# The first sweep of a four-layer graph kernel with split operands, and remainders taken by two engines

## The chip, the cores and the metric

The kernel runs on one core of one Trainium2 chip. The metric is the device time of one launch in microseconds (us): 1341.96 us, the median of three runs (1341.93 to 1343.07) of the kernel before. A profile of one further execution, of 1341.3 us, is what the traces below come from; its span, from the first instruction to the last, is 1339.5 us, so 1.8 us lie around it.

## What is computed

The input is x (4096 x 128) and a dense float32 matrix adj (4096 x 4096, 64 MB). Four graph layers follow each other, each closed by a residual and a layer norm:

```python
x = _layernorm(x + _L0_gnn_ref(x, adj, ...))   # (adj @ x + beta*x) / (rowsum(adj) + beta) @ kernel + bias
x = _layernorm(x + _L1_gnn_ref(x, adj, ...))   # h = relu(adj @ (h @ W) + b), three times, widths 20, 20, 128
x = _layernorm(x + _L2_gnn_ref(x, adj, ...))   # D^-1/2 adj D^-1/2 @ (x @ W + b), D = rowsum(adj)
x = _layernorm(x + _L3_gnn_ref(x, adj, ...))   # adj @ x + gamma * softmax((x@W_l)(x@W_r)^T) @ x @ W_h @ W_g
```

So adj is read six times: once for layer 0, three times for layer 1, once each for layers 2 and 3. The row sums of adj are needed after the first of these readings.

## The kernel before

Each reading of adj is a sweep, s = 0 to 5. A sweep has eight rows c of 512 output nodes, and a row has eight blocks d of 512 input nodes, in two halves h: a tile is 128 x 1024 float32 (512 KB), a row has 16 tiles, a sweep 128. Tiles stream through a ring `raw` of 8 slots; SyncE (SP) issues the loads, waiting for a slot with `wait_ring`. In every row two blocks (four tiles, `KEPT`) are held in SBUF through the sweeps 0 to 3 and not loaded again; only those of row 1 (`LATE`) are streamed in sweep 0 and loaded into their place afterwards by `load_late`.

Sweeps 1 to 3 are narrow (20 columns of TensorE) and share tiles: `joined` says which tiles of a sweep also serve the product of the next sweep, and such a joint tile is used twice and not read again. In sweep 0, row c has c joint blocks (all d below c), whose second product goes to the bank `ahead`, which ScalarE copies to `sums` in `store_ahead`. `FILL` names rows whose held tiles TensorE works off between the sweeps 0 and 1, where it waits for the last row's layer norm.

Sweep 0 (`first_sweep`, L1298) multiplies in plain float32: two 128x512 matmuls per tile, each recorded as two. VectorE does nothing for this product; it adds up the tiles for the row sums (`row_sum`, L867, 15 additions per row, then `fold`, L872), which TensorE sums over partitions with a column of ones (L1207). The wide sweeps 4 and 5 instead split each operand in two parts, hi and lo, of a format that TensorE multiplies faster: ScalarE copies the tile to `t_hi` (L743), VectorE subtracts (`t_lo`, L1029), and TensorE does three products per 512 columns (L1449, L1450, L1454). ScalarE may be at most HL = 4 tiles ahead of TensorE there. In the attention of layer 3, ScalarE and GpSimd split the exponentials (L799, L613) while VectorE works on scores in PSUM (L1081, L1103).

Each engine has its own in-order queue, written out by hand. The work that ends a row (its epilogue) is threaded through the next row at fixed tile numbers: TensorE's `epilogue_1` after tile 1, `epilogue_3` after 9, `epilogue_4` after 11; VectorE's residual, statistics and scales between its additions; GpSimd's three small operations per row: `bx` (L578), `xb` (L555) and the copy of the new x (L583).

## Time and profile before

| | us |
|---|---|
| median of 3 runs | 1341.96 |
| profiled execution | 1341.3 |
| its span | 1339.5 |
| TensorE (PE) busy | 1285.0 (96%) |
| VectorE (DVE) busy | 930.6 (69%) |
| ScalarE (ACT) busy | 715.7 (53%) |
| GpSimd (POOL) busy | 267.5 (20%) |
| end of the first sweep | about 291 |
| first wide matmul (sweep 4) | about 531 |

The stretches: sweep 0 up to 291 us, the narrow sweeps up to 531 us, the wide sweeps up to about 905 us, then attention. TensorE is nearly always busy, so its own durations and short waits set the end; VectorE has little to spare in the wide sweeps and much in sweep 0. TensorE's matmuls overlap in the records, so the time one costs is read from start to start, not from its duration.

### The profile page before, as it was taken

How to read it: one execution, taken by the hardware profiler on the slowest of the kernel's cores; microseconds unless marked ns; L12 is line 12 of the kernel's file. 1: busy time of each engine (PE TensorE's matmuls, PEld its weight loads, DVE VectorE, ACT ScalarE, POOL GpSimd, SP SyncE). 2: the span in 40 equal slices, each digit the busy share in tenths (PEclk: the TensorE clock that was granted, in tenths of full speed). 3: DMA queues.
4: the chain of work that ended last, by engine and by line, in shares of the span. 5: the costliest groups of instructions: out<-in, count | busy, mean ns of one | idle time of the engine just before them, and what ended most of it. 6: DMA issues, size and time to landing. Idle time of an engine off the chain costs nothing.

```text
span 1339.5 us, 17278 instructions
## 1 busy us (share of the span) xinstructions
PE 1285.0 (96%) x5911; PEld 792.2 (59%) x5911; DVE 930.6 (69%) x1207; ACT 715.7 (53%) x880; POOL 267.5 (20%) x175
## 2 busy tenths in 40 slices
PE   8999999999999899999999999998899999999987
PEld 3544444433232233778787788886677767767764
DVE  6666665551010365999999989896888788788885
...
GB/s 367 314 316 251 251 219 204 173 188 181 382 333 400 309 352 407 307 353 374 351 371 359 376 356 361 382 291 0 1 0 1 1 1 1 1 18 14 1 1 32
DMA packets 81087, 288.01 MB, mean 215 GB/s; under 512 B 9466, under 2 KB 11130, under 8 KB 81018
## 3 DMA queue, kind: packets, MB, share of 16 engines
...
q8 instruction: 41, 0.67, 0.2%
...
HBM read 284.98 MB, written 2.10 MB: 214 GB/s over the span
## 4 chain that ended last, share of the span: by engine, by line
PE 79%; DVE 8%; ACT 4%; issue 4%; DMA 3%; POOL 1%; POOLq 0%; ACTq 0%; DVEq 0%; SPq 0%
PE acc L1298 17%; PE acc L1536 7%; PE acc L1454 7%; PE acc L1388 7%; PE acc L1449 6%; PE acc L1450 6%; DMA raw<-in_adj_s 3%; DVE t_lo L1029 2%; PE rs L1306 2%; PE acc L1526 2%; PE acc L1527 2%; PE acc L1530 2%; PE e L1491 2%; PE e L1493 2%; PE rs L1491 2%
## 5 line engine op out<-in xcount | busy, mean ns | idle before, releaser
L1029 DVE TENSOR_TENSOR t_lo<-raw,t_hi 128x1024 fp32r<-128x1024 f32 x256 | 311.1, 1259 | 26.7 <-ACT t_hi L743 21.8
L743 ACT ACTIVATE t_hi<-raw 128x1024 fp32r<-128x1024 f32 x256 | 261.5, 1054 | 40.5 <-PE acc L1454 39.9
L1449 PE MATMUL acc<-t_hi,st_hi 128*128 128x512 f32 x512 | 201.9, 394 | 0.9 <-ACT t_hi L743 0.9
L1450 PE MATMUL acc<-t_hi,st_lo 128*128 128x512 f32 x512 | 199.5, 390 | 0.0
L613 POOL TENSOR_TENSOR ring_lo<-ring,p_hi 128x1024 fp32r<-128x1024 f32 x64 | 155.4, 2429 | 220.0 <-ACT p_hi L799 219.9
L1298 PE MATMUL acc<-raw,x 128*128 128x512 f32 x400 | 179.3, 597 | 0.0
L1454 PE MATMUL acc<-t_lo,st_hi 128*128 128x512 f32 x512 | 159.5, 393 | 5.8 <-DVE t_lo L1029 5.0
L1103 DVE TENSOR_TENSOR ring<-ring,e 128x1024 f32<-128x1024 f32 x128 | 154.0, 1212 | 0.1
L793 ACT ACTIVATE ring<-ring 128x1024 f32<-128x1024 f32 x128 | 134.2, 1054 | 25.0 <-DVE ring L1103 24.9
L1298 PEld LDWEIGHTS acc<-raw,x 128*128 128x128 f32 x400 | 73.7, 190 | 92.0 <-issue 92.0
L1536 PE MATMUL acc<-ring,x 128*128 128x512 f32 x256 | 120.2, 592 | 0.0
L583 POOL COPY x<-xn 128x512 f32<-128x512 f32 (+1 forms) x24 | 20.4, 850 | 485.5 <-ACT xn L683 485.5
L867 DVE TENSOR_TENSOR rsum<-rsum,raw 128x1024 f32<-128x1024 f32 x86 | 109.1, 1269 | 11.0 <-DMA raw<-in_adj_s 5.5
L1454 PEld LDWEIGHTS acc<-t_lo,st_hi 128*128 128x128 f32 x512 | 95.0, 188 | 30.7 <-DVE t_lo L1029 11.4
L1449 PEld LDWEIGHTS acc<-t_hi,st_hi 128*128 128x128 f32 x512 | 96.1, 188 | 21.8 <-DVE st_lo L877 1.3
L1450 PEld LDWEIGHTS acc<-t_hi,st_lo 128*128 128x128 f32 x512 | 96.2, 188 | 19.7 <-issue 0.2
L1081 DVE TENSOR_TENSOR peak<-e,peak 128x1024 f32<-128x1024 f32 x54 | 66.1, 1223 | 41.0 <-ACT ring L805 40.8
L892 DVE TENSOR_TENSOR at<-acc,sums 128x512 f32<-128x512 f32 x20 | 13.8, 689 | 113.7 <-PE acc L1388 87.8
L1081 DVE TENSOR_TENSOR peak<-rs,peak 128x1024 f32<-128x1024 f32 x61 | 74.5, 1222 | 24.9 <-ACT ring L805 24.6
L1388 PE MATMUL acc<-raw,h_a 128*20 128x512 f32 x384 | 81.3, 596 | 2.4 <-DMA raw<-in_adj_s 1.3
L805 ACT ACTIVATE ring<-rs 128x1024 f32<-128x1024 f32 x62 | 63.3, 1021 | 36.5 <-PE rs L1493 36.4
L1491 PE MATMUL e<-q_hi,k_hi 128*128 128x512 f32 x122 | 70.0, 573 | 3.5 <-DVE peak L1081 1.9
...
## 6 DMA issues: line engine op xcount, KB each, us to landing
...
```

The source lines that it names most:

```text
L613: nc.gpsimd.tensor_tensor(ring_lo[:, n % RING, :], slot(n), p_hi[:, m % 2, :].bitcast(F32), ALU.subtract).then_inc(pl_done, 1)
L743: nc.scalar.activation(t_hi[:, g % HL, :], raw[:, k, :], ACT.Copy).then_inc(hi_done, 1)
L793: nc.scalar.activation(slot(n), slot(n), ACT.Exp).then_inc(exped, 1)
L1029: nc.vector.tensor_tensor(t_lo[:, k, :], raw[:, slot_no(s, c, g), :], t_hi[:, k, :].bitcast(F32), ALU.subtract).then_inc(lo_done, 1)
L1081: nc.vector.tensor_tensor(peak[:, :], score_bank(t)[:, :], peak[:, :], ALU.max).then_inc(s_maxed, 1)
L1103: nc.vector.tensor_tensor(part, part, row, ALU.subtract).then_inc(subbed, 1)
L1298: m = mm(a[:, :], block_of(x0, i.d * CB + i.h * GB + j), t[:, j * CW:(j + 1) * CW], start=(n == 0 and j == 0), stop=False)
L1388: m = mm(a[k:k + H, :], h[:, b * H:(b + 1) * H], t[:, j * CW:(j + 1) * CW], start=(i.d == items[0].d), stop=(i.d == items[-1].d))
L1449: mm(a[:, :], block_of(st_h, b), hi[:, m], start=(g == 0 and j == 0), stop=False)
L1450: mm(a[:, :], block_of(st_l, b), hi[:, m], start=False, stop=False)
L1454: i = mm(a[:, :], block_of(st_h, b), lo[:, m], start=False, stop=(g == NG - 1 and j == GB - 1))
L1536: r = mm(o, block_of(x, b), slot(n)[:, u * CW:(u + 1) * CW], start=(b == 0), stop=(b == NB - 1))
```

## The change

Sweep 0 is split as sweeps 4 and 5 are. ScalarE writes `x_hi` (in four parts) and a `t0_hi` for each of the 128 tiles, a remainder `t_lo` is subtracted for each, and TensorE does three products in place of the plain one. The remainders are shared by a table `POOL_LO`: GpSimd takes 9, 10, 9, 8, 8, 6, 4, 4 of the 16 in rows 0 to 7 (58 in all), VectorE the other 7, 6, 7, 8, 8, 10, 12, 12 (70). VectorE also subtracts the four parts of `x_lo`.

The row sums of joint tiles no longer come from VectorE: the stationary operand of the joint product gets a 21st column of ones, and `epilogue_1` adds the sums that this gives by four more small products with `row_picker`. VectorE's additions fall from 15 in every row to 15, 13, 11, 9, 7, 5, 3, 1.

The split needs room, so the held tiles of rows 0 to 3 are streamed in sweep 0 and loaded again after it (16 late tiles, 4 before), and `FILL` names rows 4 and 5 in place of 0 and 2. ScalarE's 16 loads of constants, issued at the head before, now stand between the tiles 4 and 5 of its first row.

VectorE's queue for the first sweep's row 1, up to its fifth addition. Before (L867 adds a tile to the row sums, L916 and L939 are the residual):

```order
L863 TENSOR_TENSOR rsum<-raw 128x1024
L867 TENSOR_TENSOR rsum<-rsum,raw 128x1024
L900 TENSOR_TENSOR deg<-e,beta 128x4
L901 TENSOR_SCALAR dg<-sq 128x4
L903 RECIPROCAL inv<-deg 128x4
L905 RECIPROCAL dinv<-dg 128x4
L916 TENSOR_TENSOR xs<-e,inv 128x512
L867 TENSOR_TENSOR rsum<-rsum,raw 128x1024
L939 TENSOR_TENSOR xs<-xs,xb 128x512
L867 TENSOR_TENSOR rsum<-rsum,raw 128x1024
```

And of the change (L1005 is a remainder, L987 the addition):

```order
L1005 TENSOR_TENSOR t_lo<-raw,t_hi 128x1024
L983 TENSOR_TENSOR rsum<-raw 128x1024
L987 TENSOR_TENSOR rsum<-rsum,raw 128x1024 x2
L1005 TENSOR_TENSOR t_lo<-raw,t_hi 128x1024
L987 TENSOR_TENSOR rsum<-rsum,raw 128x1024
L1053 TENSOR_TENSOR deg<-e,beta 128x4
L1054 TENSOR_SCALAR dg<-sq 128x4
L1056 RECIPROCAL inv<-deg 128x4
L1058 RECIPROCAL dinv<-dg 128x4
L1069 TENSOR_TENSOR xs<-e,inv 128x512
L987 TENSOR_TENSOR rsum<-rsum,raw 128x1024
```

The remainders stand between the additions, each ahead of the addition of its tile; both kinds read two tensors in SBUF.

GpSimd's queue from its first operation on. Before (rows 0 and 1 of the sweep):

```order
L578 TENSOR_TENSOR bx<-x,beta 128x512
L555 TENSOR_TENSOR xb<-x,bias 128x512
L578 TENSOR_TENSOR bx<-x,beta 128x512
L583 COPY x<-xn 128x512
L555 TENSOR_TENSOR xb<-x,bias 128x512
```

And of the change (the same two rows):

```order
L635 TENSOR_TENSOR t_lo<-raw,t_hi 128x1024 x3
L649 TENSOR_TENSOR bx<-x,beta 128x512
L635 TENSOR_TENSOR t_lo<-raw,t_hi 128x1024 x7
L621 TENSOR_TENSOR xb<-x,bias 128x512
L635 TENSOR_TENSOR t_lo<-raw,t_hi 128x1024 x2
L649 TENSOR_TENSOR bx<-x,beta 128x512
L635 TENSOR_TENSOR t_lo<-raw,t_hi 128x1024 x5
L654 COPY x<-xn 128x512
L635 TENSOR_TENSOR t_lo<-raw,t_hi 128x1024 x3
```

The small operations stay; 19 remainders are put around them in the two rows (the last of the three shown at the end is row 2's).

ScalarE's queue at the start of the change, where the constants' loads now stand:

```order
L794 ACT_TABLE_LOAD
L794 ACTIVATE x_hi<-x 128x1024
L805 ACTIVATE t_hi<-raw 128x1024 x4
L794 ACTIVATE x_hi<-x 128x1024
L805 ACTIVATE t_hi<-raw 128x1024
L809 DMA comb<-in_comb 128x128
L809 DMA k<-in_L_gnn_kernel 128x128
```

They were ahead of everything; five tiles of the split now stand before them.

The diff, cut to its core:

```diff
-LATE = 1
-FILL = {0: (0, 1), 2: (2, 3)}
+LATE = (0, 1, 2, 3)
+FILL = {4: (4, 5), 5: (5,)}
...
-    return d in KEPT[c] and not (s == 0 and c == LATE)
+    return d in KEPT[c] and not (s == 0 and c in LATE)
...
-        mine = {1: [6, 7, 5], 2: [1, 0, 3, 2]}[s]
+        mine = {1: [6, 7], 2: [1, 0, 3, 2]}[s]
...
+PLAIN = [[n for n, i in enumerate(ITEMS[0, c]) if not i.fused] for c in range(NC)]
+POOL_LO = ((1, 2, 4, 6, 7, 9, 11, 12, 14), (0, 2, 3, 5, 7, 8, 10, 12, 13, 15), (0, 2, 4, 6, 8, 10, 11, 13, 15),
+           (0, 2, 4, 6, 8, 10, 12, 14), (0, 2, 4, 6, 8, 10, 12, 14), (0, 3, 6, 9, 12, 15), (1, 5, 9, 13), (1, 5, 9, 13))
...
+        row_folded = sums[:, 0, :]
+        row_picker = comb[:, H:HA]
...
                     if i.seq == t:
-                        sp.wait_ge(sum_done, r * NSUM + max(n, 1))
-            sp.wait_ge(pe_tile, t + 1)
+                        wait_lo(sp, c, n)
+                        if i.fused:
+                            sp.wait_ge(pe_tile, JOINT_AT[c, n])
+                        else:
+                            sp.wait_ge(sum_done, sums_through(c, n))
+                        return
...
-                for d in KEPT[LATE]:
-                    for h in range(2):
-                        sp.dma_start(kept_tile(LATE, d, h), tile(LATE, 2 * d + h)).then_inc(late_in, 16)
+                for c in reversed(LATE):
+                    for d in KEPT[c]:
+                        for h in range(2):
+                            sp.dma_start(kept_tile(c, d, h), tile(c, 2 * d + h)).then_inc(late_in[c], 16)
...
+                u = c * NG + n
+                pool.wait_ge(hi_done, u + 1)
+                nc.gpsimd.tensor_tensor(t_lo[:, u % HL, :], tile_of(0, c, ITEMS[0, c][n]),
+                                        t0_hi[:, u % HL, :].bitcast(F32), ALU.subtract).then_inc(lo_pool_done, 1)
+
+            def first_row(c):
+                for n in range(NG):
+                    if n == 1 and c > 0:
+                        if c == 1:
+                            for part in range(1, XP):
+                                pool.wait_ge(x_in[part], 16)
+                        keep_old_x(0, c - 1)
+                    if n == 5:
+                        if c > 0:
+                            pool.wait_ge(pe_acc, c)
+                            alone(pool)
+                        nc.gpsimd.tensor_tensor(blocks(bx[:, :]), blocks(cols(x, c)), spread(cols(beta, c, CB)),
+                                                ALU.mult).then_inc(S["bx"], 1)
+                    if n == 13 and c > 0:
+                        pool.wait_ge(S["norm"], done("norm", 0, c - 1))
+                        alone(pool)
+                        nc.gpsimd.tensor_copy(cols(x, c - 1), xn[:, :]).then_inc(S["xw"], 1)
...
+                act.wait_ge(x_in[part], 16)
+                nc.scalar.activation(cols(x_hi, part, NB * D // XP), cols(x, part, NB * D // XP),
+                                     ACT.Copy).then_inc(x_hi_done, 1)
+
+            def first_row(c):
+                for n, i in enumerate(ITEMS[0, c]):
+                    u = c * NG + n
+                    if c == 0 and n % (NG // XP) == 0:
+                        operand_hi(n * XP // NG)
+                    wait_tile(act, 0, c, i)
+                    if u >= HL:
+                        act.wait_ge(pe_tile, SPLIT_AT[divmod(u - HL, NG)])
+                    nc.scalar.activation(t0_hi[:, u % HL, :], tile_of(0, c, i), ACT.Copy).then_inc(hi_done, 1)
+                    if c == 0:
+                        if n == 4:
+                            for dst, src in consts:
+                                nc.scalar.dma_start(dst[:, :], src).then_inc(const_in, 16)
+                        continue
+                    if n == 2:
+                        evacuate(0, c - 1, 1 - c % 2)
+                        store_ahead(0, c - 1)
+                    if n == 4:
+                        second(0, c - 1)
+                    if n == 8:
+                        deviation(0, c - 1)
+                    if n == 10:
+                        normalise(0, c - 1)
+                    if n == 12:
+                        transposed(0, c - 1)
+                if c > 0:
+                    next_h(0, c - 1)
+
...
                 nc.scalar.dma_start(dst[:, :], src).then_inc(first_in, 16)
-            act.wait_ge(x_in[1], 16)
-            for dst, src in consts:
-                nc.scalar.dma_start(dst[:, :], src).then_inc(const_in, 16)
-            for part in range(XP):
-                act.wait_ge(x_in[part], 16)
-                nc.scalar.activation(cols(x, part, NB * D // XP), cols(x0, part, NB * D // XP),
-                                     ACT.Copy).then_inc(x_all, 1)
...
-
-            def row_sum(c, n):
-
-                mine, other = ITEMS[0, c][0], ITEMS[0, c][n + 1]
+            nc.vector.memset(h_a[:, :], 1.0).then_inc(memset_done, 1)
+
+            def row_sum(c, k):
+
...
+                if c > 0:
+                    dve.wait_ge(S["mm1"], done("mm1", 0, c) - 1)
+                nc.vector.tensor_tensor(row_folded, rsum[:, 0:CW], rsum[:, CW:2 * CW],
                                         ALU.add).then_inc(S["rr"], 1)
+
+            def operand_lo(part):
+                dve.wait_ge(x_hi_done, part + 1)
+                nc.vector.tensor_tensor(cols(x_lo, part, NB * D // XP), cols(x, part, NB * D // XP),
+                                        cols(x_hi, part, NB * D // XP).bitcast(F32), ALU.subtract).then_inc(x_lo_done, 1)
+
+            def remainder(c, n):
+                u = c * NG + n
+                dve.wait_ge(hi_done, u + 1)
+                nc.vector.tensor_tensor(t_lo[:, u % HL, :], tile_of(0, c, ITEMS[0, c][n]),
+                                        t0_hi[:, u % HL, :].bitcast(F32), ALU.subtract).then_inc(lo_done, 1)
+
+            def first_row(c):
+                for n in range(NG):
+                    if c == 0 and n % (NG // XP) == 0:
+                        operand_lo(n * XP // NG)
+                    if n not in POOL_LO[c]:
+                        remainder(c, n)
+                    if n in PLAIN[c][1:]:
...
+                        if n == 4:
+                            residual_1(0, c - 1)
...
                         mm(e0[:, b * D:(b + 1) * D], block_of(at, b), k0[:, :], start=True, stop=True)
+                    if stored(0, c):
+                        pe.wait_ge(sums_done, stored(0, c))
                     for b in range(CB):
-                        i = mm(e1[:, b:b + 1], block_of(rsum, b), ones_f[:, 0:1], start=True, stop=True)
+                        i = mm(e1[:, b:b + 1], block_of(row_folded, b), ones_f[:, 0:1], start=True,
+                               stop=not stored(0, c))
+                        if stored(0, c):
+                            i = mm(e1[:, b:b + 1], block_of(sums[:, c, :], b), row_picker, start=False, stop=True)
...
-                        pe.wait_ge(x_in[i.d * XP // NC], 16)
-                    wait_tile(pe, 0, c, i)
-                    t = tile_of(0, c, i)
+                        pe.wait_ge(x_lo_done, i.d * XP // NC + 1)
+                    hi, lo = t0_hi[:, n % HL, :], t_lo[:, n % HL, :]
+                    pe.wait_ge(hi_done, c * NG + n + 1)
                     for j in range(GB):
-                        m = mm(a[:, :], block_of(x0, i.d * CB + i.h * GB + j), t[:, j * CW:(j + 1) * CW],
-                               start=(n == 0 and j == 0), stop=False)
+                        b, m = i.d * CB + i.h * GB + j, slice(j * CW, (j + 1) * CW)
+                        mm(a[:, :], block_of(x_hi, b), hi[:, m], start=(n == 0 and j == 0), stop=False)
+                        mm(a[:, :], block_of(x_lo, b), hi[:, m], start=False, stop=False)
+                    wait_lo(pe, c, n)
+                    for j in range(GB):
+                        b, m = i.d * CB + i.h * GB + j, slice(j * CW, (j + 1) * CW)
+                        k = mm(a[:, :], block_of(x_hi, b), lo[:, m], start=False, stop=False)
...
     for j in range(4):
-        arrays["comb"][32 * j:32 * j + H] = np.eye(H, P, dtype=np.float32)
+        arrays["comb"][32 * j:32 * j + HA] = np.eye(HA, P, dtype=np.float32)
```

## Rows read from the trace of the kernel before

**Rows 1.** Windows, one row of sweep 0: us, then busy of each engine (instructions), clock, DMA

```profile
74.00:108.00 34.00, 34.00 (x120) 16.23 (x116) 23.01 (x33) 3.95 (x10) 4.17 (x3) 1.00 0.67 257
```

**Rows 2.** Timeline of TensorE in sweep 0: start, length, engine, line, instructions

```profile
6.56 9.73 PE L1298 MATMUL acc<-kept_x,x 128*128 128x512 f32 x16 [6.56 <-DMA kept_x<-in_adj_s]
...
42.76 13.98 PE L1298 MATMUL acc<-raw,x 128*128 128x512 f32 x32
56.57 0.60 PE L1245 MATMUL e<-ident,xn 128*128 128x128 f32 x4
...
75.79 0.95 PE L1207 MATMUL e<-ones_f,rsum 128*128 128x1 f32 x8
...
211.76 1.16 PE L1325 MATMUL acc<-ident,bx 128*128 128x128 f32 x8
...
290.00 1.16 PE L1325 MATMUL acc<-ident,bx 128*128 128x128 f32 x8
```

**Rows 3.** Timeline of TensorE in sweep 4: the first product of two tiles that follow

```profile
573.88 0.39 PE L1449 MATMUL acc<-t_hi,st_hi 128*128 128x512 f32 x1
...
575.24 0.39 PE L1449 MATMUL acc<-t_hi,st_hi 128*128 128x512 f32 x1
```

**Rows 4.** Timeline of GpSimd in sweep 0

```profile
36.90 1.27 POOL L555 TENSOR_TENSOR xb<-x,bias 128x512 f32<-128x512 f32 x1 [8.89 <-DMA gamma<-in_L_gnn_gamma]
38.12 1.04 POOL L578 TENSOR_TENSOR bx<-x,beta 128x512 f32<-128x512 f32 x1
...
55.74 1.08 POOL L583 COPY x<-xn 128x512 f32<-128x512 f32 x1 [16.58 <-ACT xn L683]
56.99 2.04 POOL L555 TENSOR_TENSOR xb<-x,bias 128x512 f32<-128x512 f32 x1 [0.17 <-POOL x L583]
```

**Rows 5.** Instances of VectorE's addition: ns min/median/max, starts; all, then 56.5 to 58.0

```profile
L867 DVE TENSOR_TENSOR rsum<-rsum,raw x86: 1215/1225/2103, 12.8 to 274.9; 128x1024 f32<-128x1024 f32 x86
...
L867 DVE TENSOR_TENSOR rsum<-rsum,raw x2: 1443/1773/2103, 56.5 to 58.0; 128x1024 f32<-128x1024 f32 x2
```

**Rows 6.** Timeline of GpSimd and VectorE at two places of the attention

```profile
931.53 2.40 POOL L598 TENSOR_TENSOR x<-x,ones_f 128x1024 f32<-128x1024 f32 x1
...
932.30 1.92 DVE L1069 TENSOR_TENSOR v_lo<-x,v_hi 128x256 fp32r<-128x256 f32 x1
...
1310.94 2.41 POOL L613 TENSOR_TENSOR ring_lo<-ring,p_hi 128x1024 fp32r<-128x1024 f32 x1
...
1311.91 1.99 DVE L1119 TENSOR_TENSOR xf<-o_s,xf 128x512 f32<-128x512 f32 x1
```

**Rows 7.** Instances of two lines of the attention: ns min/median/max, starts

```profile
L1119 DVE TENSOR_TENSOR xf<-o_s,xf x8: 691/693/1990, 1011.5 to 1331.8; 128x512 f32<-128x512 f32 x8
...
L613 POOL TENSOR_TENSOR ring_lo<-ring,p_hi x64: 2376/2400/2741, 951.3 to 1323.3; 128x1024 fp32r<-128x1024 f32 x64
```

**Rows 8.** The page's groups: line, engine, count, then busy us and mean ns

```profile
L743 ACT ACTIVATE t_hi<-raw 128x1024 fp32r<-128x1024 f32 x256 | 261.5, 1054 | 40.5 <-PE acc L1454 39.9
...
L1103 DVE TENSOR_TENSOR ring<-ring,e 128x1024 f32<-128x1024 f32 x128 | 154.0, 1212 | 0.1
```

**Rows 9.** Timeline of ScalarE at the start: its loads of constants and what follows

```profile
11.56 0.33 ACTq L772 DMA_DIRECT2D comb<-in_comb  x1
...
20.14 1.28 ACT L775 ACT_TABLE_LOAD   x1 [20.14 <-issue]
```

**Rows 10.** Timeline of SyncE: the late loads and the first load after them

```profile
291.19 1.75 SPq L494 DMA_DIRECT2D kept_late<-in_adj_s  x4
312.23 87.60 SPq L513 DMA_DIRECT2D raw<-in_adj_s  x58
```

**Rows 11.** Windows of three stretches, columns as in rows 1

```profile
302.00:303.00 1.00, 0.67 (x4) 0.56 (x3) 0.00 (x0) 0.24 (x1) 0.00 (x0) 0.50 0.00 0
...
430.00:440.00 10.00, 10.00 (x82) 3.25 (x78) 0.69 (x1) 1.39 (x3) 0.00 (x0) 1.00 1.03 410
...
458.00:460.00 2.00, 0.00 (x0) 0.00 (x0) 1.50 (x11) 0.24 (x2) 0.00 (x0) 1.00 1.00 338
```

191 lines of the change are left out of this document (111 added, 80 removed).

## The prediction, made before the changed kernel was run

> **What bounds the kernel now.** I read the page's engine totals first, then the windows of sweep 0, then TensorE's timeline there, and last the places where GpSimd and VectorE work at once. The windows show TensorE busy all the time in sweep 0 (34.00 of 34 us) and VectorE 23.01 us of it [rows 1]. TensorE's starts give the price of its work: 32 recorded plain matmuls, eight tiles, take from 42.76 to 56.57, so 1.73 us per tile. Rows 6 and 7 of the sweep together take from 211.76 to 290.00, 78.2 us, and the sweep ends at 291.2 [rows 2]. In sweep 4 a tile of the split form takes from 573.88 to 575.24, 1.36 us [rows 3]. So TensorE bounds sweep 0 before, and the split takes 0.37 us off each of its 128 tiles: 47 us, if TensorE goes on being the bound. The question is whether it does.
>
> **What the remainders cost.** Take a row before: 23.0 us of VectorE with 15 additions of 1.225 us [rows 1, 5], so 4.6 us are for the rest. After, a row has additions plus VectorE's remainders, 1.22 us each (both are subtractions or additions of the same shape). These are 22, 19, 18, 17, 15, 15, 15, 13 in rows 0 to 7, and row 0 has four x_lo besides. Alone that gives 27.8, 26.6, 25.3, 22.9 (three times) and 20.5 us for rows 1 to 7. TensorE's row falls by 16 x 0.37 = 5.9 us and gains, from row 2 on, the four products with row_picker, which are like the four of 75.79: 0.95, less overlap 0.85 [rows 2]. Rows 6 and 7 come to 78.2 - 11.7 + 1.7 = 68.2; a row has one joint block more than the one before it, 1.2 us by the same timeline's step, so rows 1 to 5 are about 27, 29, 30, 31, 32.5. If GpSimd's share ran freely beside VectorE's, VectorE would thus be just under or at TensorE.
>
> It does not run freely in this trace. GpSimd's xb takes 1.27 us at 36.90, where VectorE is idle, and 2.04 us at 56.99, where VectorE is adding [rows 4]. At the same moment one of VectorE's additions takes 2.10 instead of 1.225, and the one before it, which meets GpSimd's copy of 55.74, takes 1.44 [rows 5]. Each waits for the other: xb ends at 59.03, the addition started at 58.0 cannot run until about 58.9. In the attention it is the same with a long GpSimd operation: the one of 1310.94 ends at 1313.35, and VectorE's 1311.91, which is 0.69 us alone, takes 1.99 and ends just after; that of 931.53 ends at 933.93 and VectorE's of 932.30 takes until 934.22 [rows 6, 7]. The attention's other VectorE work reads one tensor in PSUM and one in SBUF, and with 64 GpSimd remainders around, its 128 instances have a mean of 1.21 us: no delay [rows 7, 8]. In sweep 0 of the change VectorE's additions and remainders all have both inputs in SBUF, and GpSimd's remainders too. The Trainium skill says why (page "SBUF — State Buffer", section "Who interferes with whom"): a VectorE instruction with two SBUF inputs uses the read port it shares with GpSimd, and whoever starts first has it for the whole instruction. By that rule the two engines' times add and sharing the remainders gains nothing; by the view that engines run side by side, sweep 0 would come out as in the first rival. The rows above agree with the rule.
>
> So a GpSimd remainder costs VectorE its own length nearly. From xb: 0.88 us lost for an operation of 1.27 us, and a remainder of 2.40 us [rows 7] is 1.13 longer: 2.0. The upper bound is the whole length, 2.4; the lower is the part that falls where VectorE waits anyway, nothing. I take 2.1, near what the rows measure.
>
> **The sum of sweep 0.** Row 0: the first tile is there at 6.56 [rows 2], one ScalarE copy of 1.05 us [rows 8] follows, so 7.6. Then 26 operations of VectorE (31.7), the fold 0.7, bx 0.9 (1.04 alone, rows 4), 9 GpSimd remainders of 2.1 (18.9): 52.2. ScalarE's 16 loads of constants take from 11.56 to 20.14, 8.6 us [rows 9]; between tiles 4 and 5 they stop t_hi for that long. ScalarE waited for the second part of x until 11.56 before; from there two copies (2.1), the loads (8.6) and the next copy (1.05) put tile 5's t_hi at 23.3. The eight VectorE operations (9.8) and three GpSimd remainders (6.3) that stand before it take from 7.6 to 23.7, so they cover the loads and I count nothing; if the engines ran side by side, 6 us of it would show. Row 0 ends at 59.8.
> Rows 1 to 5, VectorE's own time + 0.9 for bx + GpSimd's 10, 9, 8, 8, 6 remainders: 49.7, 46.4, 43.0, 40.6, 36.4, together 216.1. About 1.5 us per row of VectorE's small operations (they read PSUM or one tensor) can lie beside GpSimd's: 208.6.
> Rows 6 and 7: VectorE and GpSimd need 22.9 + 0.9 + 8.4 = 32.2 and 29.8, TensorE 68.2 for both and is the bound; with ScalarE only four tiles ahead and each remainder waiting its turn I add 1 us per row: 70.2.
> End of sweep 0: 59.8 + 208.6 + 70.2 = 338.6, against 291.2 before: 47.4 us later.
>
> **The other parts.** The loads of sweep 0 keep up: it moves the same 64 MB in more time. After it, SyncE issues 16 late loads where it issued 4, ahead of the next ring loads. Before, it issued nothing from 293 to 312.23 [rows 10]; at 410 GB/s a tile is 1.28 us [rows 11], so the 12 more take 15.4 us and fit into that gap of 19. Later the narrow sweeps are near the DMA limit, so a remnant could count: 0 to 3 us. FILL has 12 block products where it had 16, so TensorE has 0.9 us less to do while it waits for the last layer norm, and its rows 5 and 4 of sweep 1 get shorter and hide less of their own epilogues: 0 to 2 us. I take 1.5 for all of it. A second memset, the wider h_a and the 21st column cost nothing on the path: TensorE's first product waits for a tile anyway, and even in proportion to the columns the 28 joint blocks of 1.2 us would be 1.7 us longer in all. The wide sweeps and the attention are unchanged.
> Sum: 1341.3 + 47.4 + 1.5 = 1390 for an execution like the profiled one, whose time is 0.7 us below the median; so 1391.
>
> **The rivals.**
> First, the engines do not block each other here, and the kernel is faster. Row 0 is then VectorE's 32.4 us from 7.6 on, with 6 us idle behind the constants: 46.5. In rows 1 to 3 VectorE (28, 27, 25) has little to do until ScalarE has copied out the last row (two copies half as wide as a t_hi, and the t_hi itself: 0.6 + 0.6 + 1.05), which costs about 4 us a row: some 32 each. Rows 4 to 7 are TensorE's, about 31 + 32.5 + 68.2. End at 275 to 276, 15.5 us earlier, and 1341.3 - 15.5 + 1.5 = 1327. For it: the remainder of 2.40 us is short enough that 10 in a row fit beside. Against it: rows 4 to 6, three separate places. It decides if a remainder costs VectorE less than 0.9 us.
> Second, half the blocking: 1.0 us per remainder, since VectorE waits in part of each row anyway. Rows 0 to 5 have 50 of them, so rows 0 to 3 come to 49.9 (from the start), 37.2, 35.0 and 32.7, rows 4 and 5 to TensorE's 31 and 32.5, and with 70.2 for the last two the end is 288.5: 1341.3 - 2.7 + 1.5 = 1340, no change. Nothing in the rows shows such a half; the row starts, where VectorE waits for the copies, speak for a part of it.
> Third, TensorE's clock. It fell to 0.50 of full speed (1.2 GHz) at 302, after 4 us in which TensorE was mostly idle, and held 1.00 in the stretch around 458 to 460 with an idle of 3 us [rows 11]. In rows 1 to 3 of the change TensorE has 27 to 30 us of work in 43 to 50. If it fell in each gap, a tile would be 2.7 us and a row about 53 to 60: rows 1 to 4 would be 4 to 20 us longer each, 1440 in all. Against it: the gaps are short, one per tile or two.
>
> **How the numbers follow.** Forecast 0.80, first rival 0.08, second 0.07, third 0.05. The forecast's own range: 50 remainders at 2.0 to 2.4 are -5 to +15, the small operations 0 to 2.8 us a row are +-7, the constants and the narrow sweeps +8: 1378 to 1412. With part of the second rival (a remainder at 1.5 us: 30 us less) the range is 1362 to 1412. A difference of 0.2%, 2.7 us, is about what can be told from no change here: slower 0.87 (the forecast, the third, a part of the second), same 0.05 (the second), faster 0.08 (the first).
>
> **What the profile after would show.** VectorE's additions and remainders in sweep 0 with a mean well above 1.22, near 2; GpSimd's remainders near 3 us, not 2.40; sweep 0 ending near 339; TensorE waiting for `t_lo` by GpSimd and VectorE through rows 1 to 5, and hardly in rows 6 and 7; its tile at 1.36 us where it does not wait. If VectorE's mean stays at 1.23 while GpSimd is at work, the forecast is wrong and the first rival holds; if VectorE is slowed but has idle time in rows 1 to 5, the second; a clock well under 1.00 in sweep 0 speaks for the third.

## The result, and the profile after

The changed kernel takes 1424.5 us (median of four runs, 1422.7 to 1426.8), the kernel before 1342.0 (four runs): a ratio of 1.062 with a 95% interval of 1.060 to 1.064. That is 82 us slower, where 49 were forecast; the time lies above the range. The profiled execution has a span of 1420.9 us, 81.4 more than before.

Windows of the changed kernel, one per row of sweep 0, each from the first product of one row's bx to that of the next; columns as in [rows 1].

```profile
0.00:58.47 58.47, 32.45 (x97) 23.81 (x97) 53.37 (x30) 25.19 (x24) 34.39 (x16) 0.82 0.72 256
58.47:114.31 55.84, 38.48 (x142) 28.64 (x140) 52.50 (x40) 20.46 (x26) 38.23 (x15) 0.76 0.43 142
114.31:165.48 51.17, 34.96 (x161) 24.95 (x157) 43.57 (x36) 19.67 (x26) 30.87 (x13) 0.87 0.49 164
165.48:209.77 44.29, 35.08 (x169) 24.85 (x165) 36.94 (x35) 19.56 (x26) 29.06 (x12) 0.92 0.65 238
209.77:251.51 41.74, 35.30 (x176) 24.33 (x173) 35.94 (x35) 19.66 (x26) 26.28 (x11) 0.92 0.53 202
251.51:294.08 42.57, 36.19 (x184) 24.12 (x180) 33.97 (x34) 19.92 (x26) 21.13 (x9) 0.88 0.53 197
294.08:331.62 37.54, 34.67 (x192) 23.09 (x188) 29.97 (x33) 19.94 (x26) 15.53 (x7) 1.00 0.59 225
331.62:366.88 35.26, 35.26 (x200) 23.32 (x196) 23.97 (x30) 16.88 (x23) 12.08 (x6) 1.00 0.61 209
```

In [rows 1] TensorE was busy in every microsecond of a row and VectorE had a third of it free. Now only row 7 is TensorE's. In row 1 VectorE is busy 52.50 of 55.84 us with 40 recorded instructions; before it did 33 in 23.0 us. The last bx products start at 366.88, where they started at 290.00 in [rows 2]: 76.9 us of the 81.4 are lost in sweep 0.

The page's groups that answer to [rows 5, 8]: line, engine, shapes and count, then busy us and mean ns, then idle time before them.

```profile
L635 POOL TENSOR_TENSOR t_lo<-raw,t_hi 128x1024 fp32r<-128x1024 f32 x53 | 155.2, 2938 | 120.9 <-ACT t_hi L805 120.9
...
L1450 PE MATMUL acc<-t_lo,x_hi 128*128 128x512 f32 x256 | 93.6, 451 | 61.0 <-DVE t_lo L1005 53.6
...
L1005 DVE TENSOR_TENSOR t_lo<-raw,t_hi 128x1024 fp32r<-128x1024 f32 x59 | 96.1, 1646 | 28.7 <-ACT t_hi L805 28.5
...
L987 DVE TENSOR_TENSOR rsum<-rsum,raw 128x1024 f32<-128x1024 f32 x46 | 95.8, 2082 | 2.2
```

VectorE's addition of 1.225 us now has a mean of 2.08, its remainder one of 1.65; GpSimd's remainder takes 2.94 where the same shape took 2.40 in the attention [rows 7]. The timeline of GpSimd and VectorE at the start of row 1 shows how they take turns:

```profile
58.93 6.13 POOL L635 TENSOR_TENSOR t_lo<-raw,t_hi 128x1024 fp32r<-128x1024 f32 x2
60.09 2.78 DVE L994 TENSOR_TENSOR sums<-rsum 128x512 f32<-128x512 f32 x1
62.79 3.35 DVE L1005 TENSOR_TENSOR t_lo<-raw,t_hi 128x1024 fp32r<-128x1024 f32 x1
65.03 2.02 POOL L649 TENSOR_TENSOR bx<-x,beta 128x512 f32<-128x512 f32 x1
66.07 2.06 DVE L983 TENSOR_TENSOR rsum<-raw 128x1024 f32<-128x1024 f32 x1
```

The fold of 60.09, 0.69 us alone, takes 2.78; VectorE's remainder of 62.79 takes 3.35 and ends 1.1 us (about one remainder's length) after GpSimd's second one at 65.06; GpSimd's bx, 1.04 us alone [rows 4], then takes 2.02. Small operations can be held too. Two lines of VectorE with four elements per partition (ns min/median/max), the first reading two tensors, the second one:

```profile
L1119 DVE SCALAR_TENSOR_TENSOR nmr<-mv,rstd x24: 161/162/2154, 88.6 to 813.2; 128x4 f32<-128x4 f32 x24
```

```profile
L1054 DVE TENSOR_SCALAR dg<-sq x8: 155/160/2279, 73.0 to 372.0; 128x4 f32<-128x4 f32 x8
```

Their longest instances both end with a remainder of GpSimd. Beside each stands a small operation that ran at its own length while the same remainder was under way: L1053, which reads one tensor in PSUM and one in SBUF, and L1117, which reads one in SBUF:

```profile
71.86 3.43 POOL L635 TENSOR_TENSOR t_lo<-raw,t_hi 128x1024 fp32r<-128x1024 f32 x1 [4.82 <-ACT t_hi L805]
72.97 0.15 DVE L1053 TENSOR_TENSOR deg<-e,beta 128x4 f32<-128x4 f32 x1
73.04 2.28 DVE L1054 TENSOR_SCALAR dg<-sq 128x4 f32<-128x4 f32 x1
...
88.20 2.49 POOL L635 TENSOR_TENSOR t_lo<-raw,t_hi 128x1024 fp32r<-128x1024 f32 x1 [5.93 <-ACT t_hi L805]
88.37 0.17 DVE L1117 RECIPROCAL rstd<-std 128x4 f32<-128x4 f32 x1
88.57 2.14 DVE L1119 SCALAR_TENSOR_TENSOR nmr<-mv,rstd 128x4 f32<-128x4 f32 x1
```

VectorE is not always busy or held. In rows 1 to 5 it is idle 32.7 us, and 27.4 us of that are two waits for ScalarE (total, times, longest):

```profile
DVE t_lo L1005 <- ACT t_hi L805: 19.1, 5, 6.8
DVE deg L1053 <- ACT sq L752: 8.3, 3, 3.5
```

Four of the five waits for t_hi, 17.8 us, stand where rows 2 to 5 begin: ScalarE writes three t_hi of the new row, then waits for TensorE's last product of the old row, copies it out, and only then writes the next t_hi. Row 1 has no such wait. Laid over each other, the timelines of VectorE and GpSimd leave about 17 us in rows 1 to 5 in which neither works; in the rest of VectorE's idle time GpSimd works alone.

Behind sweep 0 little changed. SyncE's 16 late loads and its next ring load, which answer to [rows 10]:

```profile
368.07 1.75 SPq L562 DMA_DIRECT2D kept_t<-in_adj_s  x4
...
374.10 2.84 SPq L562 DMA_DIRECT2D kept_x<-in_adj_s  x4
390.04 10.09 SPq L579 DMA_DIRECT2D raw<-in_adj_s  x7
```

They end well before the next load is due, as forecast. The wide sweeps start at 608.4, 241.5 us after the last bx products; before it was 530.8 and 240.8. The remaining 3.8 us of the difference lie behind that point, where the two kernels have the same code: 812.5 us against 808.7. TensorE's granted clock is lower there in a few places of this execution: 0.92 and 0.74 in the 10 us from 1258.4 and from 1268.4, 1.00 at the same places before. At a third place TensorE has the same 16.16 us of work within 20, at a clock of 0.91 in this execution and 1.00 in one of the first five-row kernel below (h5):

```profile
1360.90:1380.90 20.00, 16.16 (x56) 10.50 (x55) 16.11 (x17) 17.52 (x19) 8.87 (x4) 0.91 0.00 0
```

```profile
1268.40:1288.40 20.00, 16.16 (x62) 10.47 (x61) 16.49 (x18) 17.80 (x19) 8.62 (x4) 1.00 0.00 1
```

That the clock makes the 3.8 us is likely, and not shown by an experiment.

### The profile page after: what moved, and what is told of

Same layout as the page of the kernel before. It is cut to its first block, busy times and chain, and to the rows that moved or that the text cites. A ratio compares the mean times of both kernels' runs of the same rounds, so it can differ in the third digit from the quotient of the medians.

```text
span 1420.9 us, 18453 instructions
## 1 busy us (share of the span) xinstructions
PE 1286.1 (91%) x6223; PEld 866.2 (61%) x6223; DVE 1059.0 (75%) x1226; ACT 843.3 (59%) x1008; POOL 443.7 (31%) x233
## 4 chain that ended last, share of the span: by engine, by line
PE 54%; DVE 25%; issue 9%; ACT 7%; DMA 4%; POOL 1%; SPq 0%; DVEq 0%; POOLq 0%; ACTq 0%
DVE rsum L987 8%; PE acc L1535 7%; PE acc L1601 6%; PE acc L1596 6%; PE acc L1597 6%; PE acc L1683 4%; DMA raw<-in_adj_s 3%; DVE peak L1222 3%; DVE t_lo L1005 2%; ACT ring L924 2%; DVE t_lo L1170 2%; DVE ring L1244 2%; PE rs L1540 2%; PE acc L1450 2%; ACT ring L912 2%
## 5 line engine op out<-in xcount | busy, mean ns | idle before, releaser
L1170 DVE TENSOR_TENSOR t_lo<-raw,t_hi 128x1024 fp32r<-128x1024 f32 x256 | 311.1, 1260 | 26.7 <-ACT t_hi L869 21.8
L869 ACT ACTIVATE t_hi<-raw 128x1024 fp32r<-128x1024 f32 x256 | 261.5, 1054 | 40.6 <-PE acc L1601 39.9
L635 POOL TENSOR_TENSOR t_lo<-raw,t_hi 128x1024 fp32r<-128x1024 f32 x53 | 155.2, 2938 | 120.9 <-ACT t_hi L805 120.9
L805 ACT ACTIVATE t_hi<-raw 128x1024 fp32r<-128x1024 f32 x112 | 116.2, 1056 | 98.3 <-PE acc L1450 90.5
L1450 PE MATMUL acc<-t_lo,x_hi 128*128 128x512 f32 x256 | 93.6, 451 | 61.0 <-DVE t_lo L1005 53.6
L1445 PE MATMUL acc<-t_hi,x_hi 128*128 128x512 f32 x256 | 115.4, 451 | 23.5 <-DVE x_lo L999 16.0
L672 POOL COPY x<-xn 128x512 f32<-128x512 f32 (+1 forms) x17 | 12.8, 752 | 351.3 <-ACT xn L772 351.3
L1005 DVE TENSOR_TENSOR t_lo<-raw,t_hi 128x1024 fp32r<-128x1024 f32 x59 | 96.1, 1646 | 28.7 <-ACT t_hi L805 28.5
L1446 PE MATMUL acc<-t_hi,x_lo 128*128 128x512 f32 x256 | 110.5, 432 | 0.0
L1450 PEld LDWEIGHTS acc<-t_lo,x_hi 128*128 128x128 f32 x256 | 52.1, 214 | 85.0 <-DVE t_lo L1005 65.4
L987 DVE TENSOR_TENSOR rsum<-rsum,raw 128x1024 f32<-128x1024 f32 x46 | 95.8, 2082 | 2.2
```

The lines of the kernel that those rows point to most:

```text
L635: nc.gpsimd.tensor_tensor(t_lo[:, u % HL, :], tile_of(0, c, ITEMS[0, c][n]), t0_hi[:, u % HL, :].bitcast(F32), ALU.subtract).then_inc(lo_p ...
L869: nc.scalar.activation(t_hi[:, g % HL, :], raw[:, k, :], ACT.Copy).then_inc(hi_done, 1)
L987: nc.vector.tensor_tensor(rsum[:, :], rsum[:, :], tile_of(0, c, other), ALU.add).then_inc(sum_done, 1)
L1170: nc.vector.tensor_tensor(t_lo[:, k, :], raw[:, slot_no(s, c, g), :], t_hi[:, k, :].bitcast(F32), ALU.subtract).then_inc(lo_done, 1)
L1450: k = mm(a[:, :], block_of(x_hi, b), lo[:, m], start=False, stop=False)
```

## The experiments

All start from the changed kernel unless it is said otherwise. The ledger they fill is this, in us per row (worked out from windows like those above; "1 to 5" is their sum):

| kernel | row 0 | rows 1 to 5 | row 6 | row 7 | last bx |
|---|---|---|---|---|---|
| before | 36.7 | 175.0 | 38.5 | 39.7 | 290.0 |
| changed | 58.5 | 235.6 | 37.5 | 35.3 | 366.9 |
| e1, no GpSimd remainder | 50.0 | 189.5 | 34.1 | 35.3 | 308.9 |
| e2, GpSimd writes only | 43.3 | 166.3 | 34.1 | 35.3 | 279.0 |
| e6, GpSimd reads one | 50.2 | 187.3 | 34.1 | 35.3 | 306.9 |
| e7, 25 instead of 41 in rows 1 to 5 | 57.4 | 211.1 | 34.7 | 35.3 | 338.5 |
| e9, three places | 57.8 | 236.7 | 36.2 | 35.3 | 365.9 |
| h6, five fp32 rows | 36.6 | 172.0 | 34.1 | 35.3 | 278.0 |

### All remainders on VectorE (e1)

```
-POOL_LO = ((1, 2, 4, 6, 7, 9, 11, 12, 14), (0, 2, 3, 5, ...
+POOL_LO = ((),) * 8
```

> All 128 remainders of sweep 0 on VectorE, none on GpSimd (GpSimd keeps bx, the copy of old x and the new x). Theory A (a GpSimd remainder stops VectorE for its own length, so it costs VectorE about as much as doing it itself, and in the four-tile window the two cannot lie beside each other): sweep 0 gets shorter although VectorE has 58 more operations of 1.2 us; VectorE's own work is then 51 us in row 0, 40, 37.5, 35, 33, 32.5 in rows 1 to 5 and TensorE's 34 to 35 sets rows 6 and 7, a sum of about 298, with waits at the row heads 300 to 312; whole kernel 1355 to 1368. Rival B (GpSimd's remainders are real help and the loss comes from the waits between engines alone): VectorE's busy time of 303 us in the changed kernel grows by 58 x 1.2 = 70 us less what it was blocked, sweep 0 ends at or behind 368 and the kernel is at 1424 or slower. Rival C (TensorE's clock sets it): VectorE's share falls but the granted clock stays at 0.76 to 0.92 in rows 0 to 5, and sweep 0 ends near 350.

Measured: 1359.9 us, ratio 1.014 (1.011 to 1.018). 58 more instructions on VectorE, 65 us less time. Windows of rows 1 to 3:

```profile
49.97:92.52 42.55, 31.88 (x142) 22.22 (x140) 42.27 (x51) 20.63 (x26) 4.97 (x3) 0.96 0.60 197
92.52:130.94 38.42, 31.28 (x160) 22.32 (x157) 36.22 (x46) 19.68 (x26) 3.99 (x3) 1.00 0.63 219
130.94:169.45 38.51, 32.53 (x169) 22.38 (x165) 34.00 (x44) 19.68 (x26) 3.99 (x3) 1.00 0.74 273
```

Row 1 has 51 recorded VectorE instructions in 42.27 us, where 40 took 52.50. Theory A holds in sign and size, B and C fall. The price follows: rows 1 to 5 are 46.1 us longer in the changed kernel, for 41 remainders on GpSimd; 1.12 us each, and with the 1.22 us that VectorE is spared, a GpSimd remainder costs 2.34 us of elapsed time. Its own length is 2.40. This is a mean: worked out row by row the price is 2.55, 2.64, 1.94, 1.92 and 2.66, since the waits of the rows differ as well and TensorE is busy 33.29 of the 33.93 us of row 5 here. How close it comes to 2.40 is in part chance.

VectorE waits here too, although GpSimd has no remainder. In rows 1 to 5 it is busy 173.5 of 189.5 us, and most of the 16.0 us between are the same two waits:

```profile
DVE deg L1052 <- ACT sq L751: 7.4, 4, 2.4
DVE t_lo L1004 <- ACT t_hi L804: 7.2, 4, 1.8
```

### GpSimd writes but does not read (e2)

```
-  nc.gpsimd.tensor_tensor(t_lo[...], tile, t0_hi[...], ALU.subtract)
+  if c < 6: nc.gpsimd.memset(v[:, 0:TW], 0.0); nc.gpsimd.memset(v[:, TW:2 * TW], 0.0)
+  nc.gpsimd.memset(t_lo[...], 0.0)
```

> Each of GpSimd's 58 remainders is replaced by fills with zero that read nothing from SBUF: of the remainder's place in all rows, and in rows 0 to 5 of two more 1024-wide pieces of a buffer that is not in use yet, so that GpSimd is busy about as long as before for each. Left out is the subtraction of those 58 tiles (their remainder counts as zero). Theory A (what stops VectorE is GpSimd's reading of two operands): VectorE's operations run at their own length again (t_lo and row sums near 1.2 us instead of means of 1.65 and 2.08), sweep 0 ends at 276 to 295. Rival B (a GpSimd operation of 2.4 us and more in a window of four tiles sets the pace, whoever blocks whom): VectorE's means fall but its idle time grows by as much, sweep 0 ends at 350 to 368.

Measured: 1327.4 us (one run). GpSimd is still busy for most of row 1 (31.01 of 35.85 us; 38.23 in the changed kernel, where its operations were held), and VectorE is hardly slowed. Windows of rows 1 and 4, and VectorE's remainder in the page:

```profile
43.27:79.12 35.85, 30.54 (x142) 22.66 (x140) 31.83 (x40) 20.73 (x26) 31.01 (x32) 0.95 0.69 236
...
144.74:176.58 31.84, 31.84 (x177) 23.05 (x173) 23.96 (x35) 20.34 (x27) 26.68 (x29) 1.00 0.73 281
```

```profile
L1011 DVE TENSOR_TENSOR t_lo<-raw,t_hi 128x1024 fp32r<-128x1024 f32 x59 | 72.1, 1227 | 40.9 <-ACT t_hi L811 40.6
```

The 40 instructions of row 1 that took 52.50 us take 31.83. So neither GpSimd's being busy nor the length of its work in the window of four tiles is the cause; its reading is. The whole time is that of the prediction's first rival (1327 us), which supposed no blocking. Its sweep 0 is not quite: it said 275 to 276 (its terms add up to 274), and here the sweep ends at 280, the last bx products of 278.99 included. So the equal whole is in part luck.

### GpSimd reads one operand (e6)

```
-  nc.gpsimd.tensor_tensor(t_lo[...], tile, t0_hi[...], ALU.subtract)
+  nc.gpsimd.tensor_copy(t_lo[...], t0_hi[...])
```

> GpSimd's 58 remainders are replaced by copies of t0_hi, which read one operand and write the same place; left out is the subtraction (the remainder of those 58 tiles is wrong). Theory A (a GpSimd operation holds VectorE's two-operand operations only where it itself reads two operands): VectorE's t_lo and row sums stay near 1.25 us and sweep 0 ends near 279, as with the fills. Rival B (any GpSimd read of SBUF holds them for its length): VectorE's means rise as in the changed kernel (1.65 and 2.08 us), less as far as the copy is shorter than 2.4 us, and sweep 0 ends at 310 to 368.

Measured: 1358.7 us (one run), the last bx at 306.9. The page's groups:

```profile
L635 POOL CAST t_lo<-t_hi 128x1024 fp32r<-128x1024 f32 x58 | 89.4, 1547 | 163.1 <-ACT t_hi L805 163.1
L1005 DVE TENSOR_TENSOR t_lo<-raw,t_hi 128x1024 fp32r<-128x1024 f32 x59 | 84.5, 1446 | 35.2 <-ACT t_hi L805 35.1
```

Theory A falls: the copy has a mean of 1.55 us (its shortest is 1.04), VectorE's remainder 1.45. A GpSimd operation that reads one operand in SBUF holds VectorE too, as B says, and in the mean for about its own length: rows 1 to 5 are 2.2 us shorter than in e1, so a copy costs 1.22 - 0.05 = 1.17 us against 1.04 alone. The end lies 3 us under B's 310; B had allowed for a shorter copy, but not for one this short.

### No GpSimd remainder at the rows' edges (e7)

```
-POOL_LO = (..., (0, 2, 3, 5, 7, 8, 10, 12, 13, 15), (0, 2, 4, 6, 8, 10, 11, 13, 15), ...
+POOL_LO = (..., (3, 5, 7, 8, 10, 12), (4, 6, 8, 10, 11), ...
```

> GpSimd takes no remainder among a row's first and last three tiles (rows 0 to 7: 8, 6, 5, 5, 5, 4, 2, 2 of 16 instead of 9, 10, 9, 8, 8, 6, 4, 4); VectorE does the others. In rows 1 to 5 these are 25 instead of 41. Between none (VectorE busy 173.5 us in these rows, idle 16.1) and 41 (202.9 and 32.7) a remainder on GpSimd costs 0.72 us of VectorE's busy time net. Theory A (the idle time of VectorE comes from GpSimd's remainders at the heads and ends of rows): busy about 191, idle 16 to 20, rows 1 to 5 take 207 to 211 us and sweep 0 ends at 335 to 345. Rival B (it comes with every remainder, wherever it stands): idle 26 or more, rows 1 to 5 take 217 or more, sweep 0 ends at 347 or later.

Measured: 1390.5 us (one run), the last bx at 338.5; rows 1 to 5 take 211.1, VectorE busy in 189.1 and idle in 22.0. The end fits A, the idle time lies between the two: the run does not tell them apart. Each of the 25 remainders costs (211.1 - 189.5) / 25 + 1.22 = 2.08 us, less than the 2.34 of those in the changed kernel.

### Three places instead of four (e9)

```
+HL0 = 3
-  t0_hi[:, u % HL, :] ... t_lo[:, u % HL, :]
+  t0_hi[:, u % HL0, :] ... t_lo[:, u % HL0, :]
```

> The changed kernel with three places for t0_hi and t_lo in sweep 0 instead of four, so that ScalarE may be three tiles ahead of TensorE. The work of every engine is the same. In rows 1 to 5 of the changed kernel VectorE was busy 202.9 us and idle 32.7, of that 19.1 in five waits for t_hi, one at each row's head, and 8.3 for ScalarE's square root there. Theory A (VectorE's idle time is a matter of the window: ScalarE cannot be far enough ahead to cover the last remainders, the copies out of the finished row and a GpSimd operation that stops VectorE): idle in rows 1 to 5 rises to 45 to 75 us, busy stays within 5 of 203, sweep 0 ends 15 to 50 us later, 382 to 417. Rival B (the idle time is the fixed chain at the head of a row, bx products, copy out, epilogue, whatever the window): idle stays at 30 to 38, sweep 0 ends at 365 to 375.

Measured: 1418.4 us (one run), the last bx at 365.9. VectorE's waits from 60 to 320 us (total, times, longest):

```profile
DVE t_lo L1006 <- ACT t_hi L806: 40.3, 17, 5.6
```

Neither theory fits as a whole: the time is B's (365 to 375), VectorE's idle and busy times are not, and A misses the time. VectorE is idle 44.0 us in rows 1 to 5 instead of 32.7, and busy 192.8 instead of 202.9; the sum is 236.7 instead of 235.6. With a smaller window VectorE spends as idle what it spent held by GpSimd: the timelines laid over each other have about 25 us of rows 1 to 5 in which GpSimd works and VectorE is idle, where the changed kernel has 14. The time in which neither works is about 17 us in both. So that part of VectorE's idle time is a cost, and the part beside a working GpSimd is not one of its own. The four places are not the bound.

### TensorE kept busy (e4)

```
+  if c < 6:
+      for j in range(GB):
+          mm(a[:, :], zeros_r[:, :], hi[:, j * CW:(j + 1) * CW], start=False, stop=False)
```

> In rows 0 to 5 two more products of 512 columns per tile, with a stationary of zeros, stand between the hi and the lo products, so that TensorE has fewer and shorter gaps; the sum is unchanged. At full clock they cost TensorE 0.43 us a tile, 1.79 instead of 1.36 us, 7 us a row, still below VectorE's time of the rows (42 to 58 us). Theory A (VectorE and GpSimd set the rows, the granted clock of 0.76 to 0.92 lies under that): the clock of rows 0 to 5 rises to 0.95 or more and sweep 0 ends within 5 us of 368, 363 to 375. Rival B (the slow products stand in the loop of the four-tile window, so the clock has a share of its own): sweep 0 ends 8 to 25 us earlier, 343 to 360, and the kernel is that much faster.

Measured: 1427.6 us, ratio 1.0645 (1.062 to 1.067). Windows of rows 4 and 5:

```profile
216.11:259.12 43.01, 39.92 (x209) 29.02 (x205) 34.63 (x34) 20.03 (x26) 25.24 (x10) 1.00 0.51 196
259.12:300.41 41.29, 40.81 (x216) 29.13 (x212) 29.93 (x34) 20.04 (x26) 21.81 (x9) 1.00 0.54 204
```

Rows 4 and 5 run at 1.00 instead of 0.92 and 0.88 and take 84.3 us together, as in the changed kernel. Rows 0 to 3 rose only to 0.86 to 0.93, short of the 0.95 expected, and row 3 took 49.5 us instead of 44.3, with more work for TensorE in it; the last bx products start at 373.2, 6.3 us later, within A's range. So the clock lies under VectorE and GpSimd in rows 4 and 5. For rows 0 and 1 the windows of the changed kernel say it, since VectorE is busy in all but 5.1 and 3.3 us of them. For rows 2 and 3 it is likely and not shown.

### Constants at the head of ScalarE's queue (e3)

```
+  for dst, src in consts: nc.scalar.dma_start(...)      # ahead of the first tile
```

> The 16 constant loads stand at the head of ScalarE's queue again instead of behind the fifth tile. In the changed kernel ScalarE wrote no t0_hi from 12.78 to 20.26 us while they were issued, and VectorE had no idle time then. Theory A (that stall lies under VectorE's own backlog): row 0 ends within 1.5 us of 58.5, with VectorE busy 53 us in it; the whole kernel within 3 us of 1424. Rival B (the stall holds the window of four tiles back): row 0 ends 4 to 7 us earlier, and the kernel gains as much.

Measured: 1426.5 us (one run). Row 0 ends at 65.0 instead of 58.5, which neither theory said: I had forgotten that the 16 issues now stand before the first x_hi. VectorE's start in both kernels, this one first:

```profile
12.42 1.23 DVE L998 TENSOR_TENSOR x_lo<-x,x_hi 128x1024 fp32r<-128x1024 f32 x1 [9.51 <-ACT x_hi L794]
```

```profile
6.14 1.22 DVE L999 TENSOR_TENSOR x_lo<-x,x_hi 128x1024 fp32r<-128x1024 f32 x1 [3.23 <-ACT x_hi L794]
```

From there to the end of row 0 it is 52.6 us here and 52.3 in the changed kernel. So the 7.5 us in which ScalarE issues them behind the fifth tile cost nothing that shows, as A says of the stall; its "within 1.5 us of 58.5" failed.

### The late loads alone (e5)

From the kernel before: LATE, FILL and what hangs on them.

```
-LATE = 1
-FILL = {0: (0, 1), 2: (2, 3)}
+LATE = (0, 1, 2, 3)
+FILL = {4: (4, 5), 5: (5,)}
```

> The kernel before with only the late loads of the change: the held tiles of rows 0 to 3 pass through the ring in sweep 0 and are loaded at the start of sweep 1, and the tiles computed between sweep 0 and sweep 1 are those of rows 4 and 5 instead of 0 and 2. No split, no GpSimd remainders, no ones column. Theory A (this part is worth nothing): sweep 0 ends within 2 us of 290.0, from there to the start of the wide sweeps within 2 us of 240.8, the kernel within 3 us of 1342. Rival B (the late loads cost their own time: 4 tiles more than fit in the gap between two sweeps): 3 to 8 us slower, between sweep 0's end and the wide sweeps.

Measured: 1340.6 us against 1341.1, ratio 0.9997 (0.9986 to 1.0007): nothing. Sweep 0 is the same to 0.6 us, and the way from its end to the wide sweeps to 0.5 (240.3 against 240.8).

### Without the ones column (e8)

```
-PLAIN = [[n for n, i in enumerate(ITEMS[0, c]) if not i.fused] for c in range(NC)]
+PLAIN = [list(range(NG)) for c in range(NC)]
```

> The changed kernel without the ones column: VectorE adds the joint tiles into the row sum itself, 56 more operations of 128 x 1024 (2 in row 1, 2 more in each further row, 14 in row 7). Theory A (VectorE sets the rows): each costs 1.25 us, in the rows with many GpSimd remainders up to 2.1; rows 6 and 7 leave TensorE's pace (30 + 15 = 45 and 24 + 18 = 42 us of VectorE work against 37.5 and 35.3), sweep 0 ends at 425 to 460 and the kernel takes 1480 to 1515. Rival B (the waits of the four-tile window set the rows, VectorE has slack in them): sweep 0 ends before 400.

Measured: 1453.8 us (one run), the last bx at 404.4: 37.5 us later for 56 additions, 0.67 each. The size is half of A's in the mean; rows 6 and 7 take 47.9 and 42.9 us, near the 45 and 42 that A gave them, and the end lies between A's 425 and B's 400. Row 6:

```profile
313.60:361.52 47.92, 39.18 (x184) 23.23 (x180) 47.52 (x48) 19.65 (x26) 17.26 (x7) 0.91 0.48 176
```

VectorE is busy 47.52 of 47.92 us; in rows 1 to 5 it is busy 248.6 of 254.6. There the 30 additions more, 34 us of work at 1.14 us from start to start, made the rows 19.0 us longer. The rest went into the waits: the additions need no t_hi, and the time in which neither VectorE nor GpSimd works fell from about 17 us to about 3. So this run shows that those waits were real room, and it does not speak against the two engines' reads excluding each other.

### Split only where VectorE has room (h5, h6, h7)

Five fp32 rows: x0, the operand as loaded, lies in t_lo's place until row 5; all remainders of rows 5 to 7 on VectorE.

```
+FP32_ROWS = 5
+  if c < FP32_ROWS:
+      for j in range(GB): k = mm(a, block_of(x0, ...), tile[...])
+  else: (the split, as in the changed kernel)
```

> Rows 0 to 4 of sweep 0 by plain fp32 products with a copy x0 of the operand that lies where t_lo comes later; rows 5 to 7 by the split with all 48 remainders on VectorE; x_hi by ScalarE and x_lo by VectorE during rows 1 to 4. Late loads and the ones column as in the changed kernel. Theory A (the split is worth its 0.37 us a tile where VectorE has the room, and only there): rows 0 to 4 take as in the kernel before 174.4 us together, rows 5 to 7 as in the kernel without GpSimd's remainders 33.9, 34.1 and 35.3 instead of 37.4, 38.5 and 39.7, so sweep 0 ends near 278, and the kernel at 1326 to 1331, 11 to 16 us faster than before. Rival B (the step from plain to split rows costs a stall, since VectorE's first remainder waits for the last plain row): row 5 takes 36 us or more, the kernel 1331 to 1336. Rival C (the late loads and the row sums eat it): 1338 or slower.

Measured: 1330.8 us, ratio 0.9931 (0.9908 to 0.9954), 10 us faster than before. Row 5 took 35.16 us, between A and B, rows 6 and 7 34.12 and 35.31. So the time is A's (1326 to 1331). But rows 2 to 4 took 0.9 us each more than before. TensorE's groups in the window of row 3 show where (busy us, mean ns, idle before):

```profile
L1350 PE MATMUL e<-comb,sums 128*128 128x1 f32 x8 | 1.4, 250 | 0.0
L1347 PE MATMUL e<-ones_f,sums 128*128 128x1 f32 x8 | 1.4, 240 | 0.0
```

In the same row of e5 the eight recorded products with ones_f took 1.0 us and there were none with comb. So the fp32 rows' sums went back to VectorE:

```
-PLAIN = [[n for n, i in enumerate(ITEMS[0, c]) if not i.fused] for c in range(NC)]
+PLAIN = [[n for n, i in enumerate(ITEMS[0, c]) if not i.fused or c < FP32_ROWS] for c in range(NC)]
```

> As the kernel with five fp32 rows, but the row sums of rows 0 to 4 are all on VectorE again; only rows 5 to 7 take those of joint tiles from the ones column. In the five-row kernel each epilogue with the ones column had 8 more recorded one-column products on TensorE (250 ns each and as much between), and rows 2, 3 and 4 took 34.74, 35.93 and 37.11 us instead of 33.85, 35.02 and 36.21. Theory A (the ones column costs TensorE 0.9 us a row, and VectorE's sums cost nothing where TensorE sets the row): rows 2 to 4 back to 33.85, 35.0, 36.2, sweep 0 ends at 277.5 to 279, kernel at 1326 to 1328.5. Rival B (the 0.9 us comes from elsewhere, for example the late start of loads): rows 2 to 4 unchanged, kernel at 1330 or more.

Measured: 1331.2 us, ratio 0.9916 (0.9902 to 0.9931). Windows of rows 4 to 7:

```profile
138.05:174.27 36.22, 36.22 (x136) 16.36 (x133) 21.20 (x32) 7.72 (x14) 4.67 (x3) 1.00 0.62 237
174.27:208.57 34.30, 32.94 (x177) 22.06 (x173) 32.12 (x41) 20.05 (x26) 5.20 (x3) 1.00 0.66 245
208.57:242.69 34.12, 34.12 (x192) 23.25 (x188) 27.41 (x39) 19.95 (x26) 2.96 (x3) 1.00 0.67 247
242.69:278.00 35.31, 35.31 (x200) 23.32 (x196) 22.42 (x33) 16.87 (x23) 2.95 (x3) 1.00 0.61 209
```

Rows 2 to 4 are back at 33.85, 35.03 and 36.22 and the last bx starts at 278.0 instead of 281.2, as A says. The whole did not get faster with it: this profile has the clock of 0.91 in the attention that the changed kernel's had, and takes 812.3 us from the first wide product to the end where the five-row kernel above took 807.8; the runs reach from 1326.4 to 1332.1. On the whole kernel the 3.2 us cannot be told from none.

And one fp32 row less:

```
-FP32_ROWS = 5
+FP32_ROWS = 4
```

> The same with four fp32 rows: row 4 is split too, with its 16 remainders and 8 or so row sums on VectorE. Theory A (the split pays only where VectorE's work fits under TensorE's): in the kernel without GpSimd's remainders row 4 took 36.1 us with VectorE busy 31.7, as fp32 row it takes 36.2; so the time is within 2 us of the five-row one, 1326 to 1330. Rival B (without rows 0 to 3 of backlog behind it, row 4 runs at TensorE's pace, 32.6 us of work): 3 to 4 us faster than with five rows, 1323 to 1325. Rival C (the step into the split costs more in a row where VectorE is nearly full): row 4 at 38 us or more, 1330 or slower.

Measured: 1331.0 us, ratio 0.9914 (0.9899 to 0.9929). Row 4 split takes 36.51 us with VectorE busy 34.47 of it; as fp32 row it took 36.22. The last bx products start at 277.8 instead of 278.0, and the time is the same, just over A's 1326 to 1330. Theory A: the split pays where VectorE's work fits under TensorE's, and row 4 is where that ends.

## Why the prediction was wrong

**The mechanism was right, the waits beside it were missing.** A GpSimd instruction that reads SBUF holds VectorE, and the other way round; e1 and e2 show it by taking away the remainders, and by taking away only their reads. The Trainium skill (page "SBUF — State Buffer", section "Who interferes with whom") has the rule for VectorE instructions with two SBUF inputs, and the runs agree. The operation of L1054 reads one tensor and was held as well, 2.28 us instead of 0.16; the part of the rule that the prediction used does not speak of such an operation.

**Where the 29 us went.** Sweep 0 was forecast to end 47.4 us later; the last bx products start 76.9 us later. Row 0 was right (59.8 forecast with its bx products of 1.16, and these started at 58.47), in part by luck: with 2.40 per remainder the same sum would have given 62.5. Rows 6 and 7 took 72.8 us instead of 70.2. Rows 1 to 5 took 235.6 us instead of 208.6. Those 27.0 us can be laid out by the forecast's own terms:

- VectorE's own work with bx, 130.0 forecast, is 128.4 in e2, where no remainder holds it: 1.6 less.
- The waits at the head of a row: not counted at all. This is the step that failed. In the changed kernel neither VectorE nor GpSimd works for about 17.1 us of rows 1 to 5, and in e1, without a GpSimd remainder, VectorE is idle 16.0 us there. The first rival had them, "about 4 us a row", and the forecast did not, because I thought VectorE's backlog would cover them; it did so in row 1 alone.
- "2.1 per remainder": too low. At the whole length of 2.40, the forecast's own upper bound, 41 of them are 98.4 instead of 86.1, 12.3 more. The elapsed price was 2.34 by e1 and 2.08 by e7, waits included.
- "About 1.5 us per row of VectorE's small operations can lie beside GpSimd's": what is left of the sum is 128.4 + 98.4 + 17.1 - 235.6 = 8.3 us, where the forecast had 7.5, 0.8 more. This is an estimate, a remainder of the other three and not a measurement. I took the term from the attention's instructions that read PSUM and did not look at what the small ones read; the lines of L1053, L1117, L1054 and L1119 show some held and some not.

-1.6 + 17.1 + 12.3 - 0.8 = 27.0.

How the last three share their 28.6 us depends on the price of a remainder, which no run measures by itself. That waits were missing does not: with 2.40 for each remainder and nothing beside it, the sum is 226.8 us, and 8.8 of the 235.6 are still without a term.

**The smaller steps.** The constants' loads were covered (e3). The late loads fit the gap (e5, and 0.7 us in the changed kernel against 1.5 forecast). The four products with row_picker cost 0.9 us a row, as counted. Row 7, TensorE's alone, took 35.26 us, near half of the 70.2 forecast for rows 6 and 7.

**The rivals.** The first named the right time for a kernel without blocking, in part by luck (e2). The second, half the blocking, is refuted by e1, though its sign was there: I had written that idle time of VectorE in rows 1 to 5 would speak for it. It was idle 32.7 us, and the kernel was slower than forecast. Idle time of one engine did not mean that the blocking was cheap: in a part of it GpSimd ran alone, and in the other both engines waited (e9). The third had its sign as well, a clock of 0.76 to 0.92, and cost nothing that e4 could find, which for rows 2 and 3 is a weak test.

**The range.** Its upper end came from 2.4 per remainder, +-7 for the small operations and 8 for the rest. Added up, these reach 1391 + 15 + 7 + 8 = 1421 and not the 1412 that I wrote, and the measured time lies above either; nothing in it stood for a term that was missing from the sum. The lower end was widened for a case that had no row for it.
